# Attention with its group finish deferred by one group, evictions and the causal mask moved off VectorE, and a two-engine elu stage

## What is computed

```python
q = x @ w_q.T;  k = x @ w_k.T;  v = x @ w_v.T          # x: 2048 x 2048 per batch element
sigma = elu(q) + 1
mem_out = sum over 4 memories of softmax weight * (sigma @ mem[m]) / clip(sigma . norms[m])
scores = where(causal, qh @ kh.T * 128**-0.5, -1e9)    # 16 heads of 128
local  = softmax(scores) @ vh
x = layernorm(x + (g * mem_out + (1 - g) * local) @ w_o.T)      # g = sigmoid(gate)
x = layernorm(x + bitlinear(relu(bitlinear(x, w_up))**2, w_down))
```

## Time and profile before

| | us |
|---|---|
| median of three timed runs | 3610.91 (3589.23 to 3621.11) |
| the profiled execution's own time | 3368.8 |
| its span on the slowest core (core 4) | 3367.3 |
| spans of the eight cores | 3332.5 to 3367.3 |
| A1, A2 (to the last group's finish) | 542 and 1114 |
| B0, and the load ahead of B1 | 85 and 36 |
| B1, and all that follows | 513 and 1077 |

### The profile page before, as it was taken

One profiled execution on the slowest core, in us unless ns is written; L12 is line 12 of the kernel. 1 busy time (PEld: TensorE's weight loads), 2 busy tenths in 40 slices (PEclk: granted clock), 3 DMA queues, 4 the chain that ended last, 5 costly groups with the idle time before them and its releaser, 6 DMA issues.

```text
span 3367.3 us, 37649 instructions; the slowest of 8 cores (3332.5 to 3367.3 us)
## 1 busy us (share of the span) xinstructions
PE 2349.9 (70%) x14651; PEld 1452.6 (43%) x14730; DVE 1214.8 (36%) x1601; ACT 660.7 (20%) x1120; POOL 286.9 (9%) x453
## 2 busy tenths in 40 slices
PE   0267667787887888879408999976834797254874
PEld 0022224242442424415107888853322686243763
DVE  0044442222222222232441111144542675655554
ACT  0022220302113022130210111102322222242211
POOL 4100003120211202110010010001000000000000
PEclk9998988798897988879659999977955898667897
DMA  8756554120211202110037565306410353301332
GB/s 126 131 177 178 174 170 88 13 26 1 26 13 13 26 0 26 13 13 1 0 40 89 74 80 72 51 1 116 117 42 0 101 154 97 100 1 51 109 117 100
DMA packets 194596, 229.56 MB, mean 68 GB/s; under 512 B 15091, under 2 KB 162548, under 8 KB 193396
## 3 DMA queue, kind: packets, MB, share of 16 engines
q0 software_dynamic: 134160, 109.10, 20.7%
q1 hardware_dynamic: 59108, 109.66, 11.0%
q10 hardware_dynamic: 1152, 8.39, 0.6%
HBM read 294.23 MB, written 8.39 MB: 90 GB/s over the span
## 4 chain that ended last, share of the span: by engine, by line
PE 56%; DVE 19%; DMA 15%; issue 4%; ACT 4%; POOL 2%; DVEq 1%; ACTq 0%; SPq 0%; POOLq 0%
PE ps_all L743 13%; PE ps_all L434 7%; PE ps_all L451 7%; PE ps_all L1094 7%; PE ps_all L1289 5%; DMA swst<-wdnT 4%; PE ps_all L494 4%; DMA swst<-wupT 4%; PE ps_all L499 4%; DVE denr L560 3%; PE ps_all L955 3%; PE ps_all L516 3%; DVE swpart L309 2%; PE ps_all L571 2%; DVE wdb L1252 2%
## 5 line engine op out<-in xcount | busy, mean ns | idle before, releaser
L743 PE MATMUL ps_all<-membuf,sigT 128*128 128x256 bf16 x4096 | 448.9, 273 | 38.4 <-DMA membuf<-mem 38.4
L325 PE MATMUL ps_all<-xTb,wqb 128*128 128x512 bf16 x1004 | 264.9, 422 | 256.0 <-DMA wqb<-wqT 148.2
L743 PEld LDWEIGHTS ps_all<-membuf,sigT 128*128 128x128 bf16 x4096 | 401.5, 98 | 85.6 <-issue 38.4
L1289 PE MATMUL ps_all<-wdb,rtq 128*128 128x256 bf16 x2048 | 257.4, 294 | 93.3 <-DVE wdb L1252 54.2
L325 PEld LDWEIGHTS ps_all<-xTb,wqb 128*128 128x128 bf16 x1024 | 105.6, 106 | 414.9 <-issue 328.4
L1289 PEld LDWEIGHTS ps_all<-wdb,rtq 128*128 128x128 bf16 x2048 | 214.4, 105 | 136.1 <-issue 97.0
L1094 PE MATMUL ps_all<-wub,xqT 128*128 128x256 bf16 x2048 | 256.0, 292 | 23.0 <-DVE wub L1022 9.6
L434 PE MATMUL ps_all<-xTb,kw 128*128 128x512 bf16 x1000 | 234.0, 396 | 12.8 <-DMA kw<-wkT 9.6
L1094 PEld LDWEIGHTS ps_all<-wub,xqT 128*128 128x128 bf16 x2048 | 211.7, 104 | 65.8 <-issue 29.5
L451 PE MATMUL ps_all<-vw,xTb 128*128 128x256 bf16 x2048 | 224.9, 273 | 0.0
L451 PEld LDWEIGHTS ps_all<-vw,xTb 128*128 128x128 bf16 x2048 | 200.4, 98 | 24.9
(11 more groups left out here) (160 smaller groups left out, 2156.3 us busy)
## 6 DMA issues: line engine op xcount, KB each, us to landing
swst<-wupT SPq DMA_DIRECT2D x64, 512.0 KB, 4.6
swst<-wdnT SPq DMA_DIRECT2D x64, 512.0 KB, 4.7
membuf<-mem POOLq DMA_DIRECT2D x64, 512.0 KB, 16.9
wfs<-wupT POOLq DMA_DIRECT2D x16, 1024.0 KB, 6.6
wfs<-wupT SPq DMA_DIRECT2D x16, 1024.0 KB, 6.8
wfd<-wdnT SPq DMA_DIRECT2D x16, 1024.0 KB, 6.7
wfd<-wdnT POOLq DMA_DIRECT2D x16, 1024.0 KB, 6.7
xTb<-xT POOLq DMA_DIRECT2D x64, 128.0 KB, 9.1
```

What stands on the lines that cost most here:

```text
L325: k.emit("tensor", lambda t, oc=oc, lc=lc, dc=dc, bank=bank: t.matmul(ps[bank][:, 0:CH], wqb[:, dc * D + oc * 128: dc * D + (oc + 1) * 128 ...
L743: k.emit("tensor", lambda t, ss=ss, m=m, dc=dc, bank=bank, buf=buf: t.matmul(ps[bank][:, 0:256], sigT[:, dc * OWN + ss * 128: dc * OWN + ( ...
L1289: k.emit("tensor", lambda t, ss=ss, ic=ic, bank=bank, buf=buf: t.matmul(ps[bank][:, 0:256], rtq[:, qbase(ss) + ic * 128: qbase(ss) + ic * ...
```

## The change

Five edits, all in A2 and B0:

1. The finish of a group becomes a function, `emit_group_fin`, and a queue `finq` holds it back by one group: the finish of group g is written behind the matmuls of group g+1. What is left over at the end of a head pair is written between the key and the value matmuls of the next one (and behind the last group at the very end).
2. The causal mask of the diagonal pairs is no longer a DVE multiply. The table `tri` now holds 0 and -1e9, and two matmuls per diagonal pair (identity as weights, `trib` as moving operand, 512 columns each) add it to the scores in PSUM before the Exp, which writes `expm` directly.
3. The copies of keys and values out of PSUM are made by ACT (`AF.Copy`), each waiting also for ACT's own previous instruction.
4. B0: ACT does Relu(-q) and Exp(-that), DVE only max-and-add and the row sum; the two scratch buffers hold two halves that are used in turn, so ACT may run up to two columns ahead.
5. Drains of DVE in B0 become waits on DVE's own count.

The lines of the new kernel: finish L413, L419, L425, L429, L434; keys L466 and L473; values L486 and L493; scores L553, mask L563; Exp L576 (bias) and L587 (diagonal); denominators L530, values L535; elu L620, L624, L628.

```diff
@@ A2, ahead of the loop over head pairs
-        den_bc_t = 0
+        den_bc_t = [0]
+        finq = []
+
+        def emit_group_fin(info):
+            h, o, par, pvb, dnb, pv_bank, dn_bank, att_mm = info
+            k.emit("vector", lambda v, dnb=dnb: v.reciprocal(
+                denr[0:1, 0:CH], dnb[0:1, 0:CH]),
+                waits=[(tmm, att_mm), (vve, gb_v),
+                       (tmm, den_bc_t[0])], inc=vve)
+            dn_guard_v = vve.n
+            k.drain("vector", inc=vve)
+            k.emit("vector", lambda v: v.tensor_single_scalar(
+                denr[0:1, 0:CH], denr[0:1, 0:CH], gb[0:1, 1:2],
+                ALU.mult), inc=vve)
+            k.drain("vector", inc=vve)
+            drv = vve.n
+            wts = [(vve, drv)] + bank_w(6)
+            k.emit("tensor", lambda t: t.matmul(
+                ps[6][:, 0:CH], onerf[:, :], denr[0:1, 0:CH],
+                start=True, stop=True), waits=wts, inc=tmm)
+            den_bc_t[0] = tmm.n
...
+            bank_guard[6] = (vve, vve.n)
...
+            grp_guard[par] = [(vve, vve.n)]
+            bank_guard[pv_bank] = (vve, vve.n)
+            bank_guard[dn_bank] = (vve, dn_guard_v)
@@ the copies of the keys (those of the values are changed alike)
-                    k.emit("vector", lambda v, hip=hip, st=st, bank=bank: v.tensor_copy(
+                    k.emit("scalar", lambda s, hip=hip, st=st, bank=bank: s.activation(
                         khh[:, hip * S + st * CH: hip * S + (st + 1) * CH],
-                        ps[bank][:, 0:CH]),
-                        waits=[(tmm, max(tmm.n, att_t))], inc=vve)
-                    bank_guard[bank] = (vve, vve.n)
+                        ps[bank][:, 0:CH], AF.Copy),
+                        waits=[(tmm, max(tmm.n, att_t)), (sse, sse.n)],
+                        inc=sse)
+                    bank_guard[bank] = (sse, sse.n)
             kw_t = tmm.n
+            while finq:
+                emit_group_fin(finq.pop(0))
             for ss in range(16):
@@ the scores of a diagonal pair
-                                start=True, stop=True), waits=wts, inc=tmm)
+                                start=True, stop=not diag),
+                                waits=wts, inc=None if diag else tmm)
+                        if bp[0][2] == "diag":
+                            kb0 = bp[0][1]
+                            for half in range(2):
+                                k.emit("tensor", lambda t, scb=scb, kb0=kb0, half=half: t.matmul(
+                                    psc[scb][:, half * CH:(half + 1) * CH],
+                                    idb[:],
+                                    trib[:, (kb0 + half) * CH:
+                                         (kb0 + half + 1) * CH],
+                                    start=False, stop=True),
...
-                                expp[:, slot * 1024:(slot + 1) * 1024],
+                                expm[:, slot * 1024:(slot + 1) * 1024],
...
-                            k.emit("vector", lambda v, slot=slot, kb0=kb0: v.tensor_mul(
-                                expm[:, slot * 1024:(slot + 1) * 1024],
-                                expp[:, slot * 1024:(slot + 1) * 1024],
-                                trib[:, kb0 * CH:(kb0 + 2) * CH]),
...
@@ the end of a group
                     att_mm = tmm.n
...
+                    finq.append((h, o, par, pvb, dnb, pv_bank, dn_bank,
+                                 att_mm))
+                    if len(finq) > 1:
+                        emit_group_fin(finq.pop(0))
@@ B0
         for oc in range(NCK):
-            k.emit("vector", lambda v, oc=oc: v.tensor_single_scalar(
-                scrB1[:, 0:1024], qT[:, oc * OWN:(oc + 1) * OWN], 0.0,
-                ALU.min), waits=[(vve, a1_v), (sse, ch["exp"])], inc=vve)
...
+            off = (oc % 2) * 1024
+            k.emit("scalar", lambda s, oc=oc, off=off: s.activation(
+                scrB1[:, off:off + 1024], qT[:, oc * OWN:(oc + 1) * OWN],
+                AF.Relu, scale=-1.0),
+                waits=[(vve, ch["v"].get(oc - 2, a2_v))], inc=sse)
+            k.emit("scalar", lambda s, off=off: s.activation(
+                scrB2[:, off:off + 1024], scrB1[:, off:off + 1024],
+                AF.Exp, scale=-1.0), waits=[(sse, sse.n)], inc=sse)
```

More of the change, by code:

```diff
@@ L457, in build_program @@
                         inc=tmm if dc == NCK - 1 else None)
[L458 to L462, removed]
+                k.emit("scalar", lambda s, ss=ss, bank=bank: s.activation(
+                    vpp[:, ss * 256:(ss + 1) * 256], ps[bank][:, 0:256],
+                    AF.Copy),
+                    waits=[(tmm, max(tmm.n, att_t)), (sse, sse.n)], inc=sse)
+                bank_guard[bank] = (sse, sse.n)
+            kvgen_v = (sse, sse.n)
             vw_t = tmm.n
@@ L515, in build_program @@
                                         + bank_w(scbanks[1]))
-                            k.emit("tensor", lambda t, hip=hip, h=h, o=o, pc=pc, kb=kb, scb=scb, half=half: t.matmul(
+                            diag = bp[0][2] == "diag"
+                            k.emit("tensor", lambda t, hip=hip, h=h, o=o, pc=pc, kb=kb, scb=scb, half=half, diag=diag: t.matmul(
                                 psc[scb][:, half * CH:(half + 1) * CH],
@@ L520, in build_program @@
                                 qT[:, h * OWN + o * CH: h * OWN + (o + 1) * CH],
-                                start=True, stop=True), waits=wts, inc=tmm)
+                                start=True, stop=not diag),
[9 more added lines that the diff above has]
+                                    start=False, stop=True),
+                                    waits=[(sld, tri_ld)] if half == 0 else (),
+                                    inc=tmm if half == 1 else None)
                         smm = tmm.n
@@ L607, in build_program @@
                 sigT[:, oc * OWN:(oc + 1) * OWN],
-                qT[:, oc * OWN:(oc + 1) * OWN], 0.0, scrB2[:, 0:1024],
-                ALU.max, ALU.add), waits=[(sse, ch["exp"])], inc=vve)
-            k.drain("vector", inc=vve)
+                qT[:, oc * OWN:(oc + 1) * OWN], 0.0, scrB2[:, off:off + 1024],
+                ALU.max, ALU.add), waits=[(sse, ch["e"][oc]), (vve, vve.n)],
+                inc=vve)
             k.emit("vector", lambda v, oc=oc: v.reduce_sum(
                 sbarO[:, oc:oc + 1], sigT[:, oc * OWN:(oc + 1) * OWN], AX.X),
-                inc=vve)
@@ L614, in build_program @@
-            ch["stt"] = vve.n
-        k.drain("vector", inc=vve)
+                waits=[(vve, vve.n)], inc=vve)
+            ch["v"][oc] = vve.n
+        sigT_v = vve.n
         k.emit("vector", lambda v: v.tensor_add(sbarF[:], sbarO[:],
-                                                sbarP[:, 0:NCK]), inc=vve)
-        k.drain("vector", inc=vve)
+                                                sbarP[:, 0:NCK]),
+               waits=[(vve, vve.n)], inc=vve)
         k.emit("vector", lambda v: v.tensor_add(sbarF[:], sbarF[:],
@@ L620, in build_program @@
                                                 sbarP[:, NCK:2 * NCK]),
-               inc=vve)
+               waits=[(vve, vve.n)], inc=vve)
         k.drain("vector", inc=vve)
         sbar_v = vve.n
-        sigT_v = vve.n
         wts = [(vve, sbar_v), (sld, consts_ld)] + bank_w(0)
@@ L1470, in _consts @@
         for kb in range(4):
-            tri[:, kb * CH:(kb + 1) * CH] = ((kb * 128 + p) <= q).astype(BF)
+            tri[:, kb * CH:(kb + 1) * CH] = np.where(
+                (kb * 128 + p) <= q, 0.0, -1e9).astype(BF)
         _CONSTS = {
```

61 lines of the change are left out of this document (18 added, 43 removed).

## The result

| | us |
|---|---|
| changed kernel, ten runs | median 3149.47 (3145.62 to 3157.28) |
| kernel before, ten runs (the three shown ahead of the prediction among them) | 3357.64 to 3621.11 |
| ratio, changed to before | 0.9358, interval 0.9339 to 0.9378 |
| own time of the profiled executions | 3368.8 before, 3149.1 after |

The change makes the kernel 6.4% faster.

A forecast was written before the change was run, and what follows sets the result against it. PE bounds A2, with a 4.26 us hole and slow matmuls after every group; B0 is a chain through one buffer. Gains of 200 (A2) and 25 (B0) make 225, taken from the timed median: 3610.9 - 225 = 3386 us, range 3120 to 3470.

The forecast's parts named there:

- the same 225: Whole kernel: the summed gain in us, 200 from A2 and 25 from B0.
- reserve: A2 head pair: 1.0 us added to 112 for what is imperfect, a short stretch at the lower clock.
- guard: A2, ahead of the values: PE's wait for the deferred finish's copy and multiply, 1.85 us once in a head pair.
- Rival (a): A2 groups: clock stays near 0.80, only the waits go, so 3498 us; chance 12%.
- Rival (b): A2: PE without holes gets less clock; a mean of 0.79 gives all 225 us back; chance 6%.
- Rival (c): B0: changes between Relu and Exp load tables, 1.28 us each; 4.9 a column, 3418 us in all; chance 4%.

## Why the prediction was right and where it was wrong

**The base.** The step that failed is the last one of the sum: "The timed runs lie 242 above that execution and no row shows where; I subtract the same 225 from their median: 3610.9 - 225 = 3386." The 242 us were no property of the kernel: five of its ten timed runs took 3358 to 3376 us. Three runs that agree with each other within 1% had been taken for its level, and the one profiled execution for the exception. The own time of the profiled execution minus the same 225 is 3144 us, against 3149.5 measured. The text used this value only for the low end of its range (3144 less 24) and gave the other one as the forecast, without any row for it. That the gain itself comes within 5 us of the forecast (219.7 against 225) is in part luck: A2, B0 and A1 gave some 15 us more than forecast, and the load ahead of B1 and the rest took 21 back.

**The deferral.** Right in mechanism and size. Head pair: forecast 112 from the rows (113 with a reserve), measured 112.24. Groups of 8.4 and 15.8 were 8.26 and 15.64; the broadcast of 1.0 was 1.05; keys 28.7 were 27.7, since the clock no longer falls ahead of them. The mis-sized term is the values: 1.85 of guard was right (1.77), but behind the 2.9 us of broadcast and guard the values run at a clock of 0.75 for their first 6.5 us and take 29.7, not 28.1. That is the reserve of 1 us, and the run with the finish of D inside the keys shows it: without that gap the values take 28.11. The wait at the end of A2 is 5.7 us where it was 4.3.

**The clock.** Rival (a) said the groups might stay at 0.80; they are at 1.00. Undeferring shows the size, some 82 of 200 us. The rival's own price can't be followed in one term: its 5.8 us of masks a head pair come from no row (16 x 0.265 are 4.2). Rival (b), less clock for a denser stage, fell: 0.98 in the whole stage. This trace's mean of 0.98 over 906 us, with PE busy for 856 of them and 0.99 on each of the eight cores between 800 and 1400 us, does not agree with the 13/16 that the Trainium skill gives for three cores of a die in dense matmuls (TensorE: Matmul & The Clock Gate, Part 1).

**The mask.** Forecast 34 us on PE for 31.5 of waiting: about even. PE's part was mis-sized: 0.265 was half of the 0.53 from two scores to the denominator behind them, and a mask matmul put in between adds 0.21 (0.42 for two), 27 us for 128, and 0.18 on the path when it is doubled. The waits for DVE were right (31.2). What the forecast left out is the clock: with the mask on DVE its waits are followed by slower matmuls. Net, the mask on PE gains 18 us of A2, but no total shows it.

**The copies.** Right that they are hidden on ACT, and silent on what they do for DVE: without them the fourth finish of each head pair would be 4.9 us late. The sum was not touched, since it was worked out for the queue without them.

**B0.** Forecast 2.7 per column and 45.5 in all, measured 2.65 and 44.8, the stage -26.7 against -25.5. DVE is the bound as forecast (its operations stand end to end while ACT waits 0.5 us a column for it). That a min left on DVE would make the column 3.4 with two buffers is an estimate from rows that no run tested. The prediction's 0.68 against 1.06 set a min against an Exp; the Relu took 1.06 as well. Rival (c), table loads, fell.

**The load ahead of B1.** Forecast unchanged at 36, measured 52 on the slowest core and 41 against 32 in the mean: 9 to 16 us of the gain went here. The prediction had no term for this load to change. Of its cause only the sharing of the engines by the second buffer is shown.

## What to carry to other kernels

A short chain of another engine that PE must wait for costs more than its idle time where the granted clock falls behind the wait: here each 4.3 us of idle time cost some 2.6 us more (82 / 31). Write such a chain one unit of work later in the program's order, and then look at what else stands in the queue of the engine that makes it, since everything ahead of it there becomes its delay. And before subtracting a gain from a median, ask which of two disagreeing times, the profiled execution's or the timed ones', is the kernel's: the row for a gain is no row for the level.

## What the runs showed that was not expected

- Idle time of 4.26 us was followed by matmuls at the lower level (four scores in 2.02 us). So was the 2.9 us stretch of broadcast and guard ahead of the values, in which PE was busy for 1.1 us: 0.75 in the next 6.5 us. In the changed kernel the gaps of up to 1.7 us at the starts of groups were not; these stretches had 1.00. But with the mask on DVE two short gaps near each other, 0.41 and 1.12 us at the start of a group, were followed by 0.58 for 4 us. A gap's own length does not tell what it costs.
- An fp32 broadcast matmul with one row (two instructions, 512 columns) took 1.12 us at the upper level and 2.04 at the lower.
- Loads issued earlier did not land first as a group: 7.17 MB had moved when the first 4 MB were complete.
- The elu work of two heads a head pair (Relu, Exp, max-and-add, row sum), put beside the keys on ACT and DVE, left A2 as long as it was (884.8 against 885.0 us).
